# Attention heads: the values products of two key tiles placed together, after the odd tile's second pair of scores

## The chip, the cores and the metric

The kernel runs on one core of a Trainium2 chip. The metric is device time in microseconds of one execution of the whole program; lower is better. The profile is one further execution of the same program, taken with the hardware profiler.

## What is computed

The program is a small network of six blocks over x of shape 2 x 2048 x 256: a mixture of experts, full attention, the mixture of experts again, a gated recurrence, causal attention with relative positions, and the recurrence again. The change touches only the full attention, 16 heads of 16 features in each of 2 batches, so 32 heads in all:

```python
q = x @ Wq.T * (1.0 / jnp.sqrt(jnp.asarray(D, x.dtype)))
k = x @ Wk.T
v = x @ Wv.T
scores = jnp.einsum('bqhd,bkhd->bhqk', q, k)          # S = 2048 queries and keys, Dh = 16
attn = jax.nn.softmax(scores, axis=-1)
out = jnp.einsum('bhqk,bkhd->bqhd', attn, v).reshape(B, S, D)
return out @ Wff.T + bff
```

## The kernel before

`heads_full_stage` (from L1472's loop helper to the end of the stage) goes over the 32 heads. Each head has KT = 16 key tiles of 128 keys and NQ = 4 blocks of 512 queries. Four engines each run a program of their own and meet at semaphores.

**Maxima, two heads ahead.** TensorE multiplies a tile of 128 queries with 1024 keys (`far`, L1646): two matmuls of 48 rows, one on array rows 0 to 47 and one on rows 64 to 111, into two adjacent banks of PSUM. Banks 0 to 3 make two such slots. VectorE takes the maximum of the 128x1024 result (L1742), 32 times a head; a `far` may start when VectorE has emptied the slot of two `far`s before (`m_free`). A small maximum over these (L1748), a 128x16 transpose on TensorE (`row`, L1653) and a copy on ScalarE (L1704) turn them into one row per head. SyncE writes it under the queries as a 49th contraction row.

**Scores and exponentials.** For key tile `kt` and query block `n`, `score` (L1618) multiplies 49x128 keys with 49x512 queries into one of only three banks, 4 to 6 (`bank`, `FULL_BANKS = 3`). The even blocks use array rows from 64 on, the odd ones from 0. ScalarE takes the exponential into `pT` (L1699), which has room for four key tiles. Score unit u = 4 kt + n may start when the exponential of unit u - 3 has ended (`p_ready`).

**Values products.** `weighted` (L1627) multiplies the four 128x512 blocks of exponentials of a key tile with the 128x32 values (16 features, one column of ones for the denominator, padding), each into its own 32 partitions of bank 7, and accumulates over the 16 tiles. In fp32 each of the four is two matmuls in the profile, so eight per key tile. It waits for the tile's fourth exponential. Its end raises `pv_done`, which lets ScalarE overwrite the slot in `pT` four tiles later, GpSimd copy the values of a later head (L1600), SyncE load queries and keys, and, once per head, ScalarE copy bank 7 out (`out`, L1709).

**The order on TensorE** is written out by hand in `body`, per key tile:

```python
score(i, q, kt, 3)
score(*after, 0)
far; far                      # the next two of ring
score(*after, 1)
score(*after, 2)
weighted(i, q, kt)
if left and kt == ROW_KT: row(...)      # ROW_KT = 11
```

where `after` is the next key tile (or tile 0 of the next head). So the first three scores of a tile are made during the tile before it. ScalarE's and VectorE's programs follow the order of the scores and of the `far`s. The outer loop runs over groups of four heads, the last group is written out, and the last head has no `far`s left; head 30 has only 22.

Of the kernel before, what the change touches and what calls it, by code (L numbers as in the profile page):

```python
# [1478 lines left out]
def heads_full_stage(k, ctx, V):  # L1479
# [3 lines left out]
    with ExitStack() as local:  # L1483
# [46 lines left out]
        def segment(q, left):  # L1530

            out = [(1, (q + 1) % 4, p) for p in range(AHEAD, SEG)] if left else []
            if left > 1:
                out += [(2, (q + 2) % 4, p) for p in range(AHEAD) if p != ROW_AT]
            return out
# [3 lines left out]
        with nc.Block() as block:  # L1539
# [65 lines left out]
            def _(pe):  # L1605
                def score(i, q, kt, n):
                    u = kt * NQ + n
                    b = bank(q, u)
                    if u >= FULL_BANKS:
                        pe.wait_ge(p_ready, PC + i * NS + u + 1 - FULL_BANKS)  # L1610
                    else:
                        former = max(v for v in range(NS) if bank((q + 3) % 4, v) == b)
                        pe.wait_ge(p_ready, PC - NS + i * NS + former + 1)
                    if u == 0:
                        pe.wait_ge(row_loaded[q], 32 * (i // 4 + 1 + q // 3))
                    base = TILE_ROWS * ((n + 1) % 2)
                    at = slice(base, base + PARTS_ROWS + 1)
                    nc.tensor.matmul(k.psum[:, b, :], k_sb[at, q, kt * P:(kt + 1) * P],  # L1618
                                     q_sb[at, q, n * BLK:(n + 1) * BLK], start=True, stop=True).then_inc(s_ready, 1)

                def weighted(i, q, kt):
                    pe.wait_ge(p_ready, PC + i * NS + (kt + 1) * NQ)
                    if kt == 0:
                        pe.wait_ge(vh_ready, i + 1)
                        pe.wait_ge(o_free, i + 1)
                    for j in range(NQ):
                        last = nc.tensor.matmul(k.psum[32 * j:32 * j + VP, 7, :], vh[:, q % 2, kt, :],  # L1627
                                                pT[:, kt % 4, j * BLK:(j + 1) * BLK],
                                                start=(kt == 0), stop=(kt == KT - 1), skip_group_check=True)
                    last.then_inc(pv_done, 1)  # L1630

                def far(i, q, p):
                    u = far_of(p)
                    if u == 0:
                        pe.wait_ge(qk_loaded[q], 16 * LOADS * (i // 4 + 1))
                    if p - 2 == ROW_AT:
                        pe.wait_ge(row_done, i + 1)
                    elif p >= 2:
                        pe.wait_ge(m_free, 2 + i * NF + far_of(p - 2) + 1)
                    else:  # L1640
                        pe.wait_ge(m_free, 2 + (i - 1) * NF + far_of(SEG + p - 2) + 1)
                    t, b = u // 2, slot(q, p)
                    for c in range(2):
                        at = slice(TILE_ROWS * c, TILE_ROWS * c + PARTS_ROWS)
                        lo = (u % 2) * WIDE + c * BLK
                        last = nc.tensor.matmul(k.psum[:, b + c, :], q_sb[at, q, t * P:(t + 1) * P],  # L1646
                                                k_sb[at, q, lo:lo + BLK], start=True, stop=True)
                    last.then_inc(m_ready, 1)

                def row(i, q):  # L1650
                    pe.wait_ge(mm_ready, i + 1)
                    pe.wait_ge(m_free, 2 + i * NF + NF)
                    nc.tensor.matmul(k.psum[0:KT, slot((q + 1) % 4, ROW_AT), 0:P], mm[:, q % 2, :], negI[:, :],  # L1653
                                     start=True, stop=True).then_inc(row_ready, 1)
# [13 lines left out]
                def body(i, q, left):  # L1668
                    ring = segment(q, left)
                    for kt in range(KT):  # L1670
                        score(i, q, kt, 3)
                        after = (i, q, kt + 1) if kt + 1 < KT else (i + 1, (q + 1) % 4, 0)
                        more = kt + 1 < KT or left
                        if more:
                            score(*after, 0)
                        for ahead, h, p in ring[2 * kt:2 * kt + 2]:
                            far(i + ahead, h, p)
                        if more:
                            score(*after, 1)
                            score(*after, 2)  # L1680
                        weighted(i, q, kt)
                        if left and kt == ROW_KT:
                            row(i + 1, (q + 1) % 4)

                full_heads_loop(pe, body)

            @block.scalar
# [614 lines left out]
```

## Time and profile before

| | |
|---|---|
| three runs | median 5137.71 us, 5130.94 to 5146.51 |
| profiled execution | 5147.41 us, span 5145.7 us |
| TensorE busy | 4600.3 us (89%) |
| VectorE busy | 3222.8 us (63%) |
| ScalarE busy | 2505.1 us (49%) |
| GpSimd busy | 549.0 us (11%) |
| full attention's heads | 723 to 2172 us of the span |

In the profile PE is TensorE's matmuls, PEld its weight loads, DVE VectorE, ACT ScalarE, POOL GpSimd, SP SyncE; L1627 is line 1627 of the kernel. A busy PE isn't PE at its peak, since matmuls are pipelined and their ends modelled. PEclk is the clock granted to TensorE as a share of full speed (1.00 is 2.4 GHz, 0.50 is 1.2 GHz). In a row of the timeline "x4" merges four instructions that follow each other, and the bracket at the end is idle time of the engine ahead of the row, with what ended it.

### The profile page before, as it was taken

How to read it: one execution, taken by the hardware profiler on the slowest of the kernel's cores; microseconds unless marked ns; L12 is line 12 of the kernel's file. 1: busy time of each engine (PE TensorE's matmuls, PEld its weight loads, DVE VectorE, ACT ScalarE, POOL GpSimd, SP SyncE). 2: the span in 40 equal slices, each digit the busy share in tenths (PEclk: the TensorE clock that was granted, in tenths of full speed). 3: DMA queues.
4: the chain of work that ended last, by engine and by line, in shares of the span. 5: the costliest groups of instructions: out<-in, count | busy, mean ns of one | idle time of the engine just before them, and what ended most of it. 6: DMA issues, size and time to landing. Idle time of an engine off the chain costs nothing. (4 is left out here: it accounts for less than half of the span.)

```text
span 5145.7 us, 82390 instructions
## 1 busy us (share of the span) xinstructions
PE 4600.3 (89%) x24752; PEld 2446.0 (48%) x24752; DVE 3222.8 (63%) x5811; ACT 2505.1 (49%) x4917; POOL 549.0 (11%) x536
## 2 busy tenths in 40 slices
PE   7999869999999999889998957699999999997688
PEld 6888723333333333258886534333444344343345
DVE  6655668888888888356664334476666666673132
ACT  3222327777777777613222211166666666664122
POOL 2322100000000000013322012200000000000000
PEclk9999969999999999789999988799999999998789
DMA  2000411111111111020000043443333333322401
GB/s 77 0 0 1 138 49 42 41 40 42 37 37 39 41 42 29 9 80 1 0 0 18 1 94 79 92 119 91 91 90 91 91 91 90 91 72 46 75 22 33
DMA packets 357225, 272.92 MB, mean 53 GB/s; under 512 B 218440, under 2 KB 314200, under 8 KB 350168
## 3 DMA queue, kind: packets, MB, share of 16 engines
q1 hardware_dynamic: 344536, 225.94, 17.5%
q0 software_dynamic: 12288, 41.95, 2.8%
q8 instruction: 213, 3.49, 0.3%
q14 instruction: 188, 1.54, 0.1%
HBM read 173.97 MB, written 106.95 MB: 55 GB/s over the span
## 5 line engine op out<-in xcount | busy, mean ns | idle before, releaser
L1742 DVE TENSOR_REDUCE full_tops<-psum 128x1 f32<-128x1024 f32 x1024 | 1206.7, 1219 | 254.2 <-PE psum L1646 254.0
L1699 ACT ACTIVATE full_probs<-psum 128x512 f32<-128x512 f32 x2048 | 1067.3, 603 | 356.1 <-PE psum L1618 322.1
L1203 ACT ACTIVATE big<-psum 128x512 f32<-128x512 f32 (+3 forms) x1280 | 644.7, 532 | 473.2 <-PE psum L1103 267.7
L1240 DVE TENSOR_REDUCE big<-psum 128x1 f32<-128x512 f32 (+4 forms) x1152 | 650.3, 581 | 211.6 <-PE psum L1132 201.1
L1618 PE MATMUL psum<-full_q,full_k 49*128 49x512 f32 x2048 | 665.1, 486 | 54.2 <-ACT full_probs L1699 38.3
L1618 PEld LDWEIGHTS psum<-full_q,full_k 49*128 49x128 f32 x2048 | 292.2, 191 | 655.0 <-ACT full_probs L1699 589.9
L1627 PE MATMUL psum<-full_probs,full_vh 128*32 128x512 f32 x4096 | 573.2, 633 | 0.7 <-ACT full_probs L1699 0.7
L1114 PE MATMUL psum<-big 128*32 128x512 f32 (+3 forms) x2560 | 493.8, 549 | 0.0
L1095 PE MATMUL psum<-big 97*128 97x512 bf16 (+3 forms) x1280 | 443.3, 359 | 53.9 <-ACT big L1203 39.0
L1646 PE MATMUL psum<-full_k,full_q 48*128 48x512 f32 x2048 | 406.3, 461 | 66.2 <-DMA full_k<-qk_split 39.6
L1132 PE MATMUL psum<-big 96*128 96x512 bf16 (+4 forms) x1152 | 373.9, 353 | 17.1 <-ACT big L1189 13.5
L275 POOL TENSOR_TENSOR moe_h_lo<-moe_h,moe_h_hi 128x512 fp32r<-128x512 f32 x224 | 290.2, 1296 | 664.4 <-ACT moe_h_hi L388 664.4
L312 PE MATMUL psum<-moe_x_hi,moe_w_hi 128*128 128x512 f32 x896 | 353.3, 394 | 3.9 <-DVE moe_h L454 3.8
L312 PE MATMUL psum<-moe_x_lo,moe_w_hi 128*128 128x512 f32 x896 | 351.1, 392 | 0.0
L312 PE MATMUL psum<-moe_x_hi,moe_w_lo 128*128 128x512 f32 x896 | 349.9, 391 | 0.0
L450 DVE TENSOR_TENSOR moe_ts<-psum,moe_sg 128x512 f32<-128x512 f32 x224 | 154.6, 690 | 297.0 <-ACT moe_sg L396 296.7
L388 ACT CAST moe_h_hi<-moe_h 128x512 fp32r<-128x512 f32 x224 | 138.9, 620 | 383.6 <-DVE moe_h L454 383.6
L1646 PEld LDWEIGHTS psum<-full_k,full_q 48*128 48x128 f32 x2048 | 202.9, 195 | 217.1 <-DVE full_tops L1742 149.8
L396 ACT ACTIVATE moe_sg<-psum 128x512 f32<-128x512 f32 x224 | 133.7, 597 | 261.2 <-PE psum L312 259.7
L326 PE MATMUL psum<-moe_w_hi,moe_h_hi 128*128 128x256 f32 x896 | 256.0, 286 | 2.5 <-POOL moe_h_lo L275 2.5
L326 PE MATMUL psum<-moe_w_lo,moe_h_hi 128*128 128x256 f32 x896 | 253.7, 283 | 0.0
L326 PE MATMUL psum<-moe_w_hi,moe_h_lo 128*128 128x256 f32 x896 | 253.6, 283 | 0.0
(171 smaller groups left out, 6043.4 us busy)
## 6 DMA issues: line engine op xcount, KB each, us to landing
arena<-bias_tiles SPq DMA_DIRECT2D x32, 1280.0 KB, 6.6
band_probs<-xn POOLq DMA_DIRECT2D x64, 320.0 KB, 4.8
band_probs<-xT POOLq DMA_DIRECT2D x64, 320.0 KB, 4.4
qk_split<-qkvf_parts SPq DMA_DIRECT2D x32, 512.0 KB, 4.2
full_q<-qk_split SPq DMA_DIRECT2D x64, 256.0 KB
full_k<-qk_split SPq DMA_DIRECT2D x64, 256.0 KB
big<-qk_parts SPq DMA_DIRECT2D x224, 64.0 KB
qk_parts<-big SPq DMA_DIRECT2D x32, 384.0 KB, 2.9
```

The source lines that it names most:

```text
L312: last = nc.tensor.matmul(k.psum[:, 2 * (u % 2) + kind, :], W[wp][:, e, kind, c, m * P:(m + 1) * P], (xhi, xlo)[xp][:, half, c, :], start= ...
L326: last = nc.tensor.matmul(k.psum[:, 4 + pair, t2 * D:(t2 + 1) * D], (h, h_lo)[xp][:, (half + e) % 2, c, t * P:(t + 1) * P], W[wp][:, e, 2, ...
L1095: last = nc.tensor.matmul(k.psum[:, bank, 0:hi - lo], k_sb[0:ROW + 1, q, kt * P:(kt + 1) * P], q_sb[0:ROW + 1, q, lo:hi], start=True, stop ...
L1114: last = nc.tensor.matmul(k.psum[32 * j:32 * j + VP, 7, lo - j * BLK:hi - j * BLK], vh[:, q % 2, kt, :], pT[:, kt % 4, lo:hi], start=(kt = ...
L1132: last = nc.tensor.matmul(k.psum[:, b + (c - lo) // BLK, 0:e - c], q_sb[0:ROW, q, t * P:(t + 1) * P], k_sb[0:ROW, q, c:e], start=True, sto ...
L1203: nc.scalar.activation(pT[:, kt % 4, lo:hi], k.psum[:, 4 + u % SCORE_BANKS, 0:hi - lo], ACT.Exp).then_inc(p_ready, 1)
L1240: nc.vector.reduce_max(mx[:, r, t, slot:slot + 1], src, AX_X).then_inc(m_free, 1)
L1618: nc.tensor.matmul(k.psum[:, b, :], k_sb[at, q, kt * P:(kt + 1) * P], q_sb[at, q, n * BLK:(n + 1) * BLK], start=True, stop=True).then_inc( ...
L1627: last = nc.tensor.matmul(k.psum[32 * j:32 * j + VP, 7, :], vh[:, q % 2, kt, :], pT[:, kt % 4, j * BLK:(j + 1) * BLK], start=(kt == 0), st ...
L1646: last = nc.tensor.matmul(k.psum[:, b + c, :], q_sb[at, q, t * P:(t + 1) * P], k_sb[at, q, lo:lo + BLK], start=True, stop=True)
L1699: nc.scalar.activation(pT[:, kt % 4, n * BLK:(n + 1) * BLK], k.psum[:, bank(q, u), :], ACT.Exp).then_inc(p_ready, 1)
L1742: nc.vector.reduce_max(mx[:, q % 2, u // 2, u % 2:u % 2 + 1], src, AX_X).then_inc(m_free, 1)
```

## The change

On even key tiles no values product is issued. On odd ones, at the place where `weighted(i, q, kt)` stood, those of the even tile before it and of the odd tile follow one another. Nothing else differs: the number of instructions, the buffers and the waits of each instruction are the same.

```diff
                         if more:
                             score(*after, 1)
                             score(*after, 2)
-                        weighted(i, q, kt)
+                        if kt % 2:
+                            weighted(i, q, kt - 1)
+                            weighted(i, q, kt)
                         if left and kt == ROW_KT:
                             row(i + 1, (q + 1) % 4)
```

## Rows read from the trace of the kernel before

**Rows 1.** The page's costliest groups: xcount | busy, mean ns of one | idle before.
```profile
L1742 DVE TENSOR_REDUCE full_tops<-psum 128x1 f32<-128x1024 f32 x1024 | 1206.7, 1219 | 254.2 <-PE psum L1646 254.0
L1699 ACT ACTIVATE full_probs<-psum 128x512 f32<-128x512 f32 x2048 | 1067.3, 603 | 356.1 <-PE psum L1618 322.1
...
L1627 PE MATMUL psum<-full_probs,full_vh 128*32 128x512 f32 x4096 | 573.2, 633 | 0.7 <-ACT full_probs L1699 0.7
```

**Rows 2.** Timeline of PE, one ordinary key tile, and the two passes of its values product.
```profile
1408.52 0.50 PE L1618 MATMUL psum<-full_q,full_k 49*128 49x512 f32 x2
1408.86 0.75 PE L1646 MATMUL psum<-full_k,full_q 48*128 48x512 f32 x4
1409.44 0.76 PE L1618 MATMUL psum<-full_q,full_k 49*128 49x512 f32 x2
1410.13 1.07 PE L1627 MATMUL psum<-full_probs,full_vh 128*32 128x512 f32 x8
...
1410.58 0.61 PE L1627 MATMUL psum<-full_probs,full_vh 128*32 128x512 f32 x4
...
1411.12 0.50 PE L1618 MATMUL psum<-full_q,full_k 49*128 49x512 f32 x2
```

**Rows 3.** Timeline of PEld (TensorE's weight loads), the same key tile.
```profile
1408.63 0.19 PEld L1646 LDWEIGHTS psum<-full_k,full_q 48*128 48x128 f32 x2
1409.10 0.19 PEld L1646 LDWEIGHTS psum<-full_k,full_q 48*128 48x128 f32 x2 [0.28 <-DVE full_tops L1742]
1409.21 0.19 PEld L1618 LDWEIGHTS psum<-full_q,full_k 49*128 49x128 f32 x1
1409.70 0.18 PEld L1618 LDWEIGHTS psum<-full_q,full_k 49*128 49x128 f32 x1 [0.30 <-ACT full_probs L1699]
1410.13 0.16 PEld L1627 LDWEIGHTS psum<-full_probs,full_vh 128*32 128x32 f32 x8 [0.24 <-ACT full_probs L1699]
```

**Rows 4.** Timeline of ACT, the same key tile.
```profile
1409.05 0.60 ACT L1699 ACTIVATE full_probs<-psum 128x512 f32<-128x512 f32 x1 [0.54 <-PE psum L1618]
...
1409.05 2.06 ACT L1699 ACTIVATE full_probs<-psum 128x512 f32<-128x512 f32 x4 [0.54 <-PE psum L1618]
1411.66 0.60 ACT L1699 ACTIVATE full_probs<-psum 128x512 f32<-128x512 f32 x1 [0.54 <-PE psum L1618]
```

**Rows 5.** Timeline of DVE around the same key tile.
```profile
1406.69 2.35 DVE L1742 TENSOR_REDUCE full_tops<-psum 128x1 f32<-128x1024 f32 x2 [0.47 <-PE psum L1646]
1409.30 2.35 DVE L1742 TENSOR_REDUCE full_tops<-psum 128x1 f32<-128x1024 f32 x2 [0.25 <-PE psum L1646]
```

**Rows 6.** Timeline of PE: one head, first values products of it and of the next.
```profile
1362.39 1.06 PE L1627 MATMUL psum<-full_probs,full_vh 128*32 128x512 f32 x8
...
1404.92 1.07 PE L1627 MATMUL psum<-full_probs,full_vh 128*32 128x512 f32 x8
```

**Rows 7.** Timeline: tile 11 of that head and the next tile, PE and ACT.
```profile
1391.07 1.06 PE L1627 MATMUL psum<-full_probs,full_vh 128*32 128x512 f32 x8
...
1393.58 0.50 PE L1646 MATMUL psum<-full_k,full_q 48*128 48x512 f32 x2 [0.35 <-ACT full_rows L1704]
...
1394.25 1.07 PE L1627 MATMUL psum<-full_probs,full_vh 128*32 128x512 f32 x8
...
1393.29 0.24 ACT L1704 CAST full_rows<-psum 16x128 fp32r<-16x128 f32 x1
```

**Rows 8.** Timeline of ACT and PE where the loop over four heads ends.
```profile
1444.94 0.49 PE L1618 MATMUL psum<-full_q,full_k 49*128 49x512 f32 x2
1445.36 1.07 PE L1627 MATMUL psum<-full_probs,full_vh 128*32 128x512 f32 x8
...
1456.45 1.08 ACT L1699 ACTIVATE full_probs<-psum 128x512 f32<-128x512 f32 x2 [5.37 <-issue]
```

**Rows 9.** Busy time by stretch: us; PE, PEld, DVE, ACT, POOL; PEclk, DMA share, GB/s.
```profile
1362.39:1404.92 42.53, 42.07 (x260) 15.23 (x259) 37.77 (x34) 33.78 (x68) 0.40 (x1) 1.00 0.14 42
2104.00:2127.00 23.00, 18.83 (x109) 5.61 (x101) 0.00 (x0) 18.46 (x38) 0.00 (x0) 1.00 0.03 7
2127.30:2171.00 43.70, 40.95 (x130) 10.34 (x129) 0.00 (x0) 22.00 (x44) 0.00 (x0) 0.50 0.00 1
```

**Rows 10.** Timeline of PE in the last head, which has no maxima work.
```profile
2122.23 1.06 PE L1627 MATMUL psum<-full_probs,full_vh 128*32 128x512 f32 x8
2124.83 1.06 PE L1627 MATMUL psum<-full_probs,full_vh 128*32 128x512 f32 x8
...
2127.53 1.94 PE L1627 MATMUL psum<-full_probs,full_vh 128*32 128x512 f32 x8
2129.39 1.22 PE L1618 MATMUL psum<-full_q,full_k 49*128 49x512 f32 x3
...
2131.59 1.94 PE L1627 MATMUL psum<-full_probs,full_vh 128*32 128x512 f32 x8
```

## The prediction, made before any run of the change

> **What bounds the kernel now.** I began with the page's costliest groups. In the heads VectorE's maxima are busy 1207 us, ScalarE's exponentials 1067 us, the values products 573 us [rows 1]; VectorE and ScalarE both have idle time in front of them that ends with a TensorE score or maximum product. So neither streams freely. The timeline of one key tile tells why. Tiles follow each other every 2.60 us (1408.52 to 1411.12 [rows 2]), though four exponentials need only 2.06 us from first start to last end, or four steps of 0.49 = 1.95 us ((2.06 - 0.60)/3 = 0.49 [rows 4]), and two maxima 2.35 us [rows 5].
>
> The reader should see a ring. The exponential of (kt,3) starts at 1409.05 and ends at 1409.65 [rows 4]. The third score of the next tile, which needs its bank, loads at 1409.70 [rows 3] (+0.05), the values product loads at 1410.13 [rows 3] (+0.43), the next score stands at 1411.12 [rows 2] (+0.99) and its exponential at 1411.66 [rows 4] (+0.54). With 0.60 for the exponential that is 0.05 + 0.43 + 0.99 + 0.54 + 0.60 = 2.61 us, the spacing measured. The last head shows the same spacing with no maxima work at all (2122.23 to 2124.83 [rows 10]), so this ring, not TensorE's work and not VectorE, sets the pace. ScalarE has three exponentials in hand when the values product is coming: they last 3 x 0.49 = 1.46 us after 1409.65, and the product ends at 1411.12, 1.47 us after it. The cover is used up to the last 0.01 us, and the 0.54 that follows is ScalarE's idle time.
>
> VectorE has its own limit nearby: two slots. It idles 0.25 us a tile [rows 5], and the second maximum product of a tile already waits for it (end 1406.69 + 2.35 = 1409.04, load 1409.10 [rows 5, 3]).
>
> **What the change does, step by step.** No instruction is added or removed; eight matmuls move behind six score and maxima instructions of a later tile.
>
> 1. *The double block.* One product occupies TensorE 0.99 us up to the next load; its second pass starts 0.45 after the first (1410.13, 1410.58) and the next load comes 0.54 after that [rows 2]. If the second product follows like another pass, the block takes 0.99 + 2 x 0.44 = 1.87 us; at worst 2 x 0.99 = 1.98. I take 1.87, since the weights of all eight matmuls are loaded within 0.16 us [rows 3], ahead of the second pass.
>
> 2. *ScalarE's ring over two tiles.* In the odd tile: 0.05 + 0.43 + 1.87 + 0.54 + 0.60 = 3.49 us from one fourth exponential to the next, for the cover is still three banks, 1.46 us, against 1.87. In the even tile no product stands in the way and ScalarE runs at its own pace, 4 x 0.49 = 1.96. Sum 5.45, against 5.21 before. What is gained in the even tile (0.65) is less than what is lost in the odd (0.88).
>
> 3. *VectorE's ring, which is longer still.* Count from the load of the even tile's first maximum product, x. Its reduction starts at x + 0.67 (1408.63 to 1409.30 [rows 3, 5]); the two reductions end at x + 3.02. Only then is the slot free for the odd tile's second maximum product: load at x + 3.08 (0.06 as above). TensorE is in order, so the odd tile's scores 1 and 2 and the double block stand behind it. Scores: + 0.34 (1409.10 to 1409.44 [rows 3, 2]); double block: + 0.32 to 0.42 after the first of two scores that stand together (1444.94 to 1445.36, 0.42; from the second of them, some 0.1 later, 0.32 [rows 8]). Here both have array rows of their own and start together, so I take 0.33. Then 1.87, and 0.11 from the score's load to the next maximum product's (1408.52 to 1408.63 [rows 2, 3]). Sum 3.08 + 0.34 + 0.33 + 1.87 + 0.11 = 5.73 us for two tiles, 0.52 over 5.21. The fourth exponential of the odd tile is ready by about x + 2.97 (score wait and steps of 0.49 laid out from x + 0.43), so it isn't late. Bounds: 5.45, if VectorE's ring doesn't bite, and 5.73 + 0.09 + 0.11 = 5.93.
>
> 4. *Count.* Heads 0 to 30 have 31 x 8 = 248 pairs. Around each of seven loop ends TensorE is stalled by ScalarE (5.37 us of issue [rows 8]) and then slow, about two pairs each, where I count 0.3 instead of 0.52: 234 x 0.52 + 14 x 0.3 = 126 us.
>
> 5. *Head ends and the row.* A head takes 42.53 us [rows 6], of which 16 x 2.605 = 41.68 are tiles; tile 11 takes 3.18 (1391.07 to 1394.25), 0.57 over, for the row copy on ScalarE at 1393.29 [rows 7], and the remaining 0.28 is ScalarE's copy of bank 7 at the head's end. With ScalarE's ring 0.28 shorter than VectorE's, the copy is hidden: about -0.22 x 24 = -5 us. The row copy now delays a far product that has slack; between nothing and 0.35 a head, I take -0.15 x 31 = -5. The load queue on SyncE, GpSimd's copy of the values and the storing wait for a head's last `pv_done`, which stands where it was. The even product's slot in `pT` comes free a tile later, but the exponentials that need it are the third tile on: hidden.
>
> 6. *Last head.* Before it runs mostly at half clock (4.06 us a tile, 2127.53 to 2131.59 [rows 10]). A double block in place of two takes away one drain; between -5 and +5, I take 0.
>
> 7. *The clock.* In ordinary heads TensorE is busy 42.07 of 42.53 us and the granted clock is 1.00, 2.4 GHz; in the last head it was busy 18.83 of 23.0 us, kept 2.4 GHz that long, then fell to 0.50, 1.2 GHz, and stayed, busy or not (40.95 of 43.70) [rows 9]. The new pair has 1.87 us of dense products and then 5.73 - 1.87 = 3.86 us with four pairs of maxima products and the scores, broken by waits for exponentials and for VectorE: thinner than any stretch of an ordinary head, about as thin as the last head. So I expect some falls. A fall costs (4.06 - 2.60) = 1.46 us a tile at low clock, and two to three tiles pass until recovery, as after a loop end: about 3.5 us. Bounds: none, 0; one in every head and more, 100 us. I take ten, 35 us, the low side, because the dense block comes back every pair.
>
> Sum: 126 - 5 - 5 + 0 + 35 = **+151 us**. Against the profiled execution's 5147.4 us this is 5298; it lies 9.7 us above the median of the three runs, so the median should come to about **5288 us**.
>
> The skill bears on step 1. The Trainium skill, "TensorEngine Tiling (Array Packing)", Tiling Modes, says that changing the tiling mode drains TensorE. The trace agrees in kind: 0.54 against 0.45. By that rule alone the change saves a drain at either end of a block and the result would be that of the first rival below.
>
> **Rivals.**
>
> *Faster: TensorE's own work bounds.* TensorE is 99% busy by its records [rows 9]. Grouping spares a switch into and out of the block, 0.12 us at the exit (0.99 + 0.87 against 1.98) and about 0.1 at the entry. If the banks and slots bridged the double block, 256 x 0.22 = 56 us would go: 5138 - 56 = 5082. It decides once the cover after the third score is at least 1.87 us. Against it: the cover is 1.46 us [rows 4], and the last head with less TensorE work is no faster [rows 10]. Chance 0.06.
>
> *No difference.* The tiles' spacing is elastic in a way that the single tile doesn't show, and loss and gain cancel: 5138. Chance 0.03.
>
> *Milder: only ScalarE's ring counts.* 5.45 a pair: 248 x 0.24 = 60, with the items of step 5: about 5190. Needs the odd tile's second maximum product to find its slot free. Against: it already waits in the trace before. Chance 0.08.
>
> *Worse: the clock keeps falling.* At 1.2 GHz a double block takes 1.87 + 1.70 = 3.57 us (one is 1.86: 2127.53 to 2129.39 [rows 10]; a further one without drain 1.70). VectorE's ring then gives some 8.4 us a pair. If half the pairs ran so, 124 x 2.7 = 335 us more: about 5590. For it: step 7 and the last head, where the clock never came back. Against: ordinary heads recovered within a few tiles. Chance 0.07. The Trainium skill, "TensorE: Matmul & The Clock Gate", A second HAM failure mode: psum-queue depth-cycling, describes a kernel whose waits between groups of matmuls make the clock swing. No ordinary head of this trace shows it, the last one shows the fall.
>
> **How the numbers follow.** The forecast has the remaining 0.76. Its ends: 126 becomes 234 x 0.38 = 89 if the pair is 5.59, and 234 x 0.72 = 168 at 5.93; the clock adds 0 to 100. So +79 to +258: 5217 to 5396. The range also takes in the milder rival: 5185 to 5400, leaving out the faster side and the bad clock. A measurement of this kernel tells about 0.3% (15 us) from no change. Faster 0.06, same 0.03, slower 0.91.
>
> **What would show it.** Right: pairs of blocks of 16 values matmuls some 5.7 us apart, each 1.87 us long; VectorE idle about 1.1 us before the even tile's first maximum; the odd tile's second maximum product waiting for VectorE; ScalarE with four to five exponentials in a row, then a gap of 0.9; head ends with no extra pause; 42.5 us a head becomes about 46. Step 1 is wrong if the two products are 0.99 apart, step 3 if the pair is 5.45 and the load doesn't wait for VectorE, step 7 if the granted clock in ordinary heads stays 1.00 or swings in each of them. The whole is wrong if pairs come at 5.2 us or less.

## The result and the profile after

The changed kernel takes 5501.74 us (median, 5501.49 to 5504.1) against 5142.11 us of the kernel before in the same series: ratio 1.0713, interval 1.069 to 1.0736. The forecast was slower, 5288 us, at most 5400: the direction held, the size didn't. All ratios below are of undisturbed executions; one execution of the warm kernel's second series took 8482.83 us and stands in none.

The page's costliest groups of the changed kernel, as in [rows 1] (its lines have moved by two: L1744 is the reduction, L1701 the exponential):

```profile
L1744 DVE TENSOR_REDUCE full_tops<-psum 128x1 f32<-128x1024 f32 x1024 | 1189.8, 1216 | 633.9 <-PE psum L1646 633.2
L1701 ACT ACTIVATE full_probs<-psum 128x512 f32<-128x512 f32 x2048 | 1061.8, 610 | 683.4 <-PE psum L1618 643.7
L1627 PE MATMUL psum<-full_probs,full_vh 128*32 128x512 f32 x4096 | 733.0, 853 | 0.0
```

VectorE's and ScalarE's work is within 1.4% of what it was, and their idle time in front of it has grown by 380 and 327 us, nearly all of it waiting for TensorE. The third line tells more: a values matmul lasts 853 ns on average in place of 633. The filled kernel below issues its values matmuls in the same order, and there they last 651: order explains little of it, a slower clock the rest.

The heads' stage as one stretch of the busy-time view (us; PE, PEld, DVE, ACT, POOL; PEclk, DMA share, GB/s), first of the kernel before:

```profile
727.00:2172.40 1445.40, 1382.65 (x8157) 498.53 (x8159) 1158.51 (x1013) 1081.29 (x2105) 12.01 (x30) 0.95 0.12 36
```

and of the changed kernel:

```profile
728.60:2534.40 1805.80, 1662.43 (x8149) 600.22 (x8151) 1138.97 (x1011) 1074.05 (x2101) 12.02 (x30) 0.82 0.10 28
```

The stage is 360 us longer, which is the whole difference. The mean granted clock went from 0.95 to 0.82. With two levels, 1.00 and 0.50, the time at 1.2 GHz is 2 x (1 - PEclk) x length: 2 x 0.05 x 1445 = 145 us before, 2 x 0.18 x 1806 = 650 us after. Below this is called low-clock time. PEclk is rounded to two places, so such a time can be off by 14 to 18 us.

Two pairs of tiles that follow each other in the timeline of PE of the changed kernel show both effects at once:

```profile
1317.14 0.50 PE L1646 MATMUL psum<-full_k,full_q 48*128 48x512 f32 x2 [0.29 <-DVE full_tops L1744]
1317.47 0.40 PE L1618 MATMUL psum<-full_q,full_k 49*128 49x512 f32 x2
1317.81 1.92 PE L1627 MATMUL psum<-full_probs,full_vh 128*32 128x512 f32 x16
1319.66 0.50 PE L1618 MATMUL psum<-full_q,full_k 49*128 49x512 f32 x2
1320.00 0.63 PE L1646 MATMUL psum<-full_k,full_q 48*128 48x512 f32 x4
1320.47 1.85 PE L1618 MATMUL psum<-full_q,full_k 49*128 49x512 f32 x4
1321.91 0.65 PE L1646 MATMUL psum<-full_k,full_q 48*128 48x512 f32 x2
1322.85 0.50 PE L1646 MATMUL psum<-full_k,full_q 48*128 48x512 f32 x2 [0.29 <-DVE full_tops L1744]
1323.19 0.42 PE L1618 MATMUL psum<-full_q,full_k 49*128 49x512 f32 x2
1323.54 3.54 PE L1627 MATMUL psum<-full_probs,full_vh 128*32 128x512 f32 x16
1327.01 0.50 PE L1618 MATMUL psum<-full_q,full_k 49*128 49x512 f32 x2
```

The double block of 1317.81 holds TensorE 1.85 us (to the score at 1319.66), and the next starts 1323.54 - 1317.81 = 5.73 us later; that is the ring of the forecast. The second block is the same work at the low clock: 1327.01 - 1323.54 = 3.47 us. The busy-time view gives the clock, first around another slow double block (1303.44, 3.28 us), then for 5.71 us that hold the fast one of 1317.81, at 2.4 GHz all through:

```profile
1303.00:1306.40 3.40, 3.40 (x20) 0.59 (x16) 1.79 (x2) 1.08 (x2) 0.00 (x0) 0.50 0.13 53
1317.14:1322.85 5.71, 5.42 (x32) 2.13 (x33) 4.61 (x5) 4.13 (x9) 0.00 (x0) 1.00 0.04 14
```

Over the second block itself, 1323.54 to 1327.01, PEclk is 0.52. The weight load of the odd tile's second maxima product shows the wait that step 3 of the forecast rests on, 0.73 us (PEld, of which 0.29 are left in PE's row):

```profile
1317.14 0.19 PEld L1646 LDWEIGHTS psum<-full_k,full_q 48*128 48x128 f32 x2 [0.73 <-DVE full_tops L1744]
```

VectorE's timeline shows its side of the ring, to be held against [rows 5]:

```profile
1314.73 4.61 DVE L1744 TENSOR_REDUCE full_tops<-psum 128x1 f32<-128x1024 f32 x4 [2.61 <-PE psum L1646]
1320.44 4.61 DVE L1744 TENSOR_REDUCE full_tops<-psum 128x1 f32<-128x1024 f32 x4 [1.10 <-PE psum L1646]
1327.79 2.36 DVE L1744 TENSOR_REDUCE full_tops<-psum 128x1 f32<-128x1024 f32 x2 [2.74 <-PE psum L1646]
```

Four reductions without a break, then idle for 1.10 us when the double block ran at 2.4 GHz and for 2.74 when it ran at 1.2. Of the 256 blocks of the stage about 50 follow their predecessor after 5.7 us; most others take 6.0 to 8.2. Counted in the timeline, 177 of the 256 double blocks hold TensorE for more than 1.95 us, 3.24 on average, the others 1.84. So about seven pairs of tiles in ten pay.

### The profile page after: what moved, and what is told of

Its sections match the earlier page's. It is cut to its first block and busy times, and to the rows that moved or that the text cites. A ratio compares the mean times of both kernels' runs of the same rounds, so it can differ in the third digit from the quotient of the medians.

```text
span 5502.4 us, 82390 instructions
## 1 busy us (share of the span) xinstructions
PE 4876.2 (89%) x24752; PEld 2544.2 (46%) x24752; DVE 3206.8 (58%) x5811; ACT 2499.4 (45%) x4917; POOL 549.0 (10%) x536
## 3 DMA queue, kind: packets, MB, share of 16 engines
q8 instruction: 212, 3.47, 0.3%
## 5 line engine op out<-in xcount | busy, mean ns | idle before, releaser
L1744 DVE TENSOR_REDUCE full_tops<-psum 128x1 f32<-128x1024 f32 x1024 | 1189.8, 1216 | 633.9 <-PE psum L1646 633.2
L1701 ACT ACTIVATE full_probs<-psum 128x512 f32<-128x512 f32 x2048 | 1061.8, 610 | 683.4 <-PE psum L1618 643.7
L1618 PE MATMUL psum<-full_q,full_k 49*128 49x512 f32 x2048 | 740.0, 494 | 76.8 <-ACT full_probs L1701 66.8
L1627 PE MATMUL psum<-full_probs,full_vh 128*32 128x512 f32 x4096 | 733.0, 853 | 0.0
L1618 PEld LDWEIGHTS psum<-full_q,full_k 49*128 49x128 f32 x2048 | 323.3, 197 | 626.1 <-ACT full_probs L1701 367.5
L1646 PE MATMUL psum<-full_k,full_q 48*128 48x512 f32 x2048 | 486.3, 467 | 125.5 <-DVE full_tops L1744 66.5
L1646 PEld LDWEIGHTS psum<-full_k,full_q 48*128 48x128 f32 x2048 | 215.3, 198 | 258.3 <-DVE full_tops L1744 174.2
L1627 PEld LDWEIGHTS psum<-full_probs,full_vh 128*32 128x32 f32 x4096 | 137.1, 139 | 375.1 <-issue 198.2
```

What stands on the lines that cost most here:

```text
L1701: nc.scalar.activation(pT[:, kt % 4, n * BLK:(n + 1) * BLK], k.psum[:, bank(q, u), :], ACT.Exp).then_inc(p_ready, 1)
L1744: nc.vector.reduce_max(mx[:, q % 2, u // 2, u % 2:u % 2 + 1], src, AX_X).then_inc(m_free, 1)
```

## The experiments

The theory behind them: the double block outlasts ScalarE's three banks and puts VectorE's second slot ahead of it, which makes a pair of tiles 5.73 us (some 130 us in all); the rest, some 230 us, is the clock, which falls because TensorE's work between double blocks is thin. The rivals were the delay itself, the banks alone, VectorE alone, and a clock with no part in it.

### A tile later, but one by one

```diff
-                        if kt % 2:
-                            weighted(i, q, kt - 1)
-                            weighted(i, q, kt)
+                        if kt:
+                            weighted(i, q, kt - 1)
+                        if kt == KT - 1:
+                            weighted(i, q, kt)
```

> Every values product is issued one key tile later than before the change, at the same place in the order, each by itself; only at a head's end do two stand together. Theory (it is the double block, not the delay, that costs: TensorE is away for 1.87 us where ScalarE has 1.46 us in hand, and the clock falls over the thin stretch between blocks): tiles stay 2.60 us apart, one double block a head adds 0.5 to 3 us, so 5155 to 5240 us. Rival (the delay itself costs, by the slots of the exponentials or by pv_done): 5400 or more, with ScalarE waiting for a values product. Rival (nothing but the number of blocks matters): 5142.

Measured: 5192.72 us, ratio to before 1.0099 (1.007 to 1.0127). The tiles stand 2.60 us apart, as in this timeline of PE:

```profile
1401.00 1.07 PE L1627 MATMUL psum<-full_probs,full_vh 128*32 128x512 f32 x8
...
1403.60 1.06 PE L1627 MATMUL psum<-full_probs,full_vh 128*32 128x512 f32 x8
```

So a product issued a tile late doesn't lengthen a tile; neither the slots of the exponentials nor `pv_done` hold one up. The 1% goes with the one double block of each head: PEclk of the stage is 0.91, 268 us of low clock against 145, and 23 of the 24 falls of the clock in this stage begin 4.6 to 7.2 us behind the start of a double block (six of these blocks stand at loop ends, where the clock fell before the change too).

### The same delay, the blocks apart

In odd tiles, with the change's pair taken apart:

```diff
-                        for ahead, h, p in ring[2 * kt:2 * kt + 2]:
+                        for ahead, h, p in ring[2 * kt:2 * kt + 1]:
                             far(i + ahead, h, p)
+                        if kt % 2:
+                            weighted(i, q, kt - 1)
+                        for ahead, h, p in ring[2 * kt + 1:2 * kt + 2]:
+                            far(i + ahead, h, p)
...
                         if kt % 2:
-                            weighted(i, q, kt - 1)
                             weighted(i, q, kt)
```

> The even tile's values product is issued in the odd tile as in the change, but between the odd tile's two maxima products, in TensorE's wait for VectorE, and the odd tile's own product where it was before. The same delay, the same 16 matmuls for two tiles, two blocks of 0.99 us. Theory: two tiles take about 5.4 us at 2.4 GHz, and the work is spread, so the clock falls seldom: 5190 to 5270 us. Rival (the change costs through ScalarE's banks alone, wherever the blocks stand): as the change, 5450 to 5510. Rival (the delay costs): 5450 or more.

Measured: 5221.5 us, ratio 1.0174 (1.0135 to 1.0213). Timeline of PE, one pair:

```profile
1401.86 1.07 PE L1627 MATMUL psum<-full_probs,full_vh 128*32 128x512 f32 x8
...
1405.69 1.06 PE L1627 MATMUL psum<-full_probs,full_vh 128*32 128x512 f32 x8
1406.68 0.50 PE L1646 MATMUL psum<-full_k,full_q 48*128 48x512 f32 x2
...
1407.35 1.06 PE L1627 MATMUL psum<-full_probs,full_vh 128*32 128x512 f32 x8
```

A pair takes 1407.35 - 1401.86 = 5.49 us (5.4 expected), more than two single tiles, yet the kernel is 280 us faster than the changed one: 0.28 us more a pair, 248 times, is 69 of the 77 us over the kernel before, and PEclk is back at 0.95. The same sixteen matmuls, as late, cost about a fifth as much when they are spread.

### More work in the wait

The changed kernel with repeats of one maxima product, which fill TensorE's 0.73 us wait for VectorE in the odd tile. The semaphore is raised by the last copy.

```diff
-                    for c in range(2):
+                    for c in [0, 1] * copies:
...
-                        for ahead, h, p in ring[2 * kt:2 * kt + 2]:
-                            far(i + ahead, h, p)
+                        for at, (ahead, h, p) in enumerate(ring[2 * kt:2 * kt + 2]):
+                            far(i + ahead, h, p, 3 if kt % 2 and at == 0 else 1)
```

> The changed kernel, with the odd tile's first maxima product issued three times into the same banks (two further pairs of matmuls with the same result), in the 0.73 us in which TensorE waits there for VectorE. More work, none of it on VectorE's or ScalarE's ring. Theory (some 230 of the 360 us are the granted clock, which falls because the stretch between two double blocks is thin): pairs of tiles at 2.4 GHz stay 5.7 us, low clock falls from 650 us of the stage to under 300, time 5380 to 5450 us. Rival (the clock has no part, the rings make it all): 5502 or up to 30 us more. Rival (what counts is the double block's own density, not the thin stretch): low clock unchanged, 5500 to 5530.

Measured: 5297.7 us, ratio 1.0308 (1.0278 to 1.0338). Nearly a thousand matmuls more in the stage, and 204 us less than the changed kernel. The timeline of PE:

```profile
1402.59 1.44 PE L1646 MATMUL psum<-full_k,full_q 48*128 48x512 f32 x8
1403.86 0.40 PE L1618 MATMUL psum<-full_q,full_k 49*128 49x512 f32 x2
1404.19 1.92 PE L1627 MATMUL psum<-full_probs,full_vh 128*32 128x512 f32 x16
...
1409.89 1.92 PE L1627 MATMUL psum<-full_probs,full_vh 128*32 128x512 f32 x16
```

The ring is untouched, 1409.89 - 1404.19 = 5.70 us, and the double block stays at full speed. The gain beat the expectation (5380 to 5450). Its page has the values products at 542.1 us, against 733.0 of the changed kernel; the 191 us between are nearly the whole gain:

```profile
L1627 PE MATMUL psum<-full_probs,full_vh 128*32 128x512 f32 x4096 | 542.1, 651 | 0.0
```

The same values products in the same order, only faster: this shows that the clock is the larger part. The stage:

```profile
726.90:2330.10 1603.20, 1516.96 (x9128) 680.06 (x9127) 1156.79 (x1011) 1075.75 (x2101) 12.02 (x30) 0.94 0.11 32
```

Low clock is 2 x 0.06 x 1603 = 192 us against 650, and the stage is 203 us shorter: 0.44 us lost per us at low clock.

Where the clock still falls supports the theory. Of the 41 double blocks that are still over 1.95 us, 7 stand in the last head, which has no copies, 15 around the ends of heads, and 19 directly behind the row of tile 11, where the pair has a further wait, 0.58 us for ScalarE's copy of the row, that nothing fills. Of the 155 double blocks of tiles 3 to 11 in the other heads not one is slow; in the changed kernel 112 are.

### Half the filling

`2` in place of `3` copies.

> The filled kernel with one extra copy in place of two: half of the filling. Theory (low clock follows how full the thin stretch is): between changed and filled, low clock 250 to 500 us, 5310 to 5430 us, pairs at 2.4 GHz 5.7 us. Rival (a threshold that two copies pass and one doesn't): 5490 to 5510.

Measured: 5426.53 us, ratio 1.057 (1.0546 to 1.0594). In the stage:

```profile
728.00:2452.00 1724.00, 1625.47 (x8637) 647.17 (x8639) 1155.59 (x1011) 1075.88 (x2101) 12.02 (x30) 0.86 0.10 30
```

Low clock 2 x 0.14 x 1724 = 483 us. Against the filled kernel that is 291 us more of it and 121 us more time, 0.42 per us; against the changed kernel 167 us less of it and 82 us less time, 0.49. The price stays between 0.42 and 0.49. One copy gives 75 us, the second 129.

### The same work in the dense place

`3 if kt % 2 == 0 and at == 0 else 1`: the copies stand behind the double block.

> The changed kernel with the same extra work as the filled one (one maxima product of each pair of tiles issued three times), but that of the even tile, which stands right behind the double block where TensorE is dense already, and not in the wait for VectorE. Theory (the clock falls for the thin stretch between the blocks, and the wait in it is what filling cures): the copies add up to 2 x 0.24 us a pair of tiles to the ring and leave the waits where they are, so low clock stays over 450 us of the stage and the time is 5480 to 5620 us. Rival (more work anywhere keeps the clock up): low clock about 200 us as in the filled kernel, 5290 to 5420 us.

Measured: 5506.22 us, ratio 1.0722 (1.0699 to 1.0745), the same as the changed kernel's. The stage:

```profile
729.00:2538.20 1809.20, 1588.04 (x9131) 675.32 (x9131) 1134.19 (x1011) 1095.82 (x2101) 12.01 (x30) 0.88 0.10 28
```

Low clock is 2 x 0.12 x 1809 = 434 us, which the rounding of PEclk doesn't tell from the 450 expected, and far over the 192 of the filled kernel, with the same number of matmuls. So the place of the work matters more than its amount. The amount counts too: it took a third off the low-clock time. It gave nothing back in us: these copies stand on the ring, and pairs at 2.4 GHz take 6.17 us in place of 5.71, some 110 us in 248 pairs, against 216 x 0.44 = 95 us from the clock.

### VectorE with half its work, before and after

In either kernel the maximum goes over the first 512 of each 1024 keys; the other half is left out.

```diff
-                    src = k.psum[:, b:b + 2, :].rearrange("p b n -> p (b n)")
+                    src = k.psum[:, b, :]
```

> The changed kernel with the maximum taken over only the first 512 of each 1024 keys, which leaves out half of VectorE's work (about 0.6 us a reduction instead of 1.22). Theory (VectorE's two slots make two tiles 5.7 us; without that ScalarE's ring of 5.45 is left): pairs at 2.4 GHz 5.4 to 5.5 us, and the thin stretch has no wait for VectorE; 5340 to 5440 us in all. Rival (ScalarE's banks alone set the 5.7): pairs stay 5.7, time 5500. Rival (VectorE is the whole of the loss): pairs 5.2, time 5150 to 5200.

> The kernel before, with the maximum taken over only the first 512 of each 1024 keys, which leaves out half of VectorE's work. Theory (before the change ScalarE's three banks alone set the 2.60 us of a tile, VectorE's slots don't): tiles stay at 2.60 us and the time within 15 us of the kernel before, 5127 to 5150 us. Rival (VectorE bounds the tile): tiles of 2.4 us or less, 5040 to 5090 us.

The changed kernel takes 5307.86 us so (ratio 1.0332, 1.0304 to 1.036), the one before 5139.85 us (1.0012, 0.9998 to 1.0026). Timeline of PE, changed kernel with half the maxima:

```profile
1401.78 1.92 PE L1627 MATMUL psum<-full_probs,full_vh 128*32 128x512 f32 x16
...
1407.21 1.92 PE L1627 MATMUL psum<-full_probs,full_vh 128*32 128x512 f32 x16
```

and the kernel before with half of them:

```profile
1402.29 1.07 PE L1627 MATMUL psum<-full_probs,full_vh 128*32 128x512 f32 x8
...
1404.90 1.07 PE L1627 MATMUL psum<-full_probs,full_vh 128*32 128x512 f32 x8
```

Before the change VectorE sets nothing: 2.61 us a tile with half its load. After it a pair goes from 5.73 to 5.43 us; ScalarE's ring, put at 5.45, is what is left. The time fell further than the 5340 to 5440 expected, since low clock is down to 2 x 0.11 x 1604 = 353 us. The stage is 202 us shorter, of which the ring gives 0.30 x 248 = 74 and the clock, at the price above, 297 x 0.44 = 131. That the clock holds better because the wait for VectorE is gone fits the theory, but here the pair is shorter as well, and this run can't part the two.

```profile
727.40:2331.30 1603.90, 1516.15 (x8148) 614.50 (x8151) 636.62 (x1010) 1052.66 (x2101) 12.01 (x30) 0.89 0.11 32
```

### Keeping the kernel before warm

If work in a wait is free and holds the clock, the kernel before has two places for it: behind each end of the loop over four heads, where ScalarE stands still 5.37 us [rows 8], and the last head [rows 9, 10]. The warm kernel issues one maxima product 18 times in the first and one idle pair of matmuls a tile in the second:

```diff
-                            far(i + ahead, h, p)
+                            far(i + ahead, h, p, 18 if q == 0 and kt == 1 and at == 1 else 1)
...
                             score(*after, 1)
+                            if not left:
+                                idle(q)
                             score(*after, 2)
```

> The kernel before, with TensorE kept busy in its two idle places: the second maxima product of key tile 1 of every first head of four is issued 18 times (in the 4.5 us in which ScalarE stands still at the loop's end), and each tile of the last head has one idle pair of maxima matmuls into banks that nobody reads, in its wait for a bank. Theory (what the clock costs is the thin stretches, and work in a wait is free): no low clock after loop ends, 3 to 5 us less at each of 7, and tiles of the last head 2.6 in place of 4.06 us, 15 us less: 5090 to 5120 us. Rival (the clock doesn't follow such filling, or the copies delay VectorE): 5142 to 5170 us.

Measured: 5115.57 us, ratio 0.9966 (0.9953 to 0.9979). The expectation of no low clock did not hold: the profiled execution (5136.98 us, no better than the kernel before) fell behind some loop ends and ran the last head at 0.50 to its end, though TensorE was now busy 99% of it by its records:

```profile
2102.80:2168.00 65.20, 64.51 (x224) 20.36 (x227) 0.00 (x0) 33.40 (x65) 0.00 (x0) 0.50 0.01 3
```

So its successor has two idle pairs a tile where the real ones had stood, from head 30's tile 12 on:

```diff
+                        if not ring[2 * kt:] and (left == 0 or kt > ROW_KT):
+                            idle(q)
+                            idle(q)
```

> As the warm kernel, but where no maxima products are left (head 30 from tile 12 on and head 31) two idle pairs of maxima matmuls stand in each tile, where the real ones stood, so that TensorE's order is that of an ordinary tile. Theory (the last head falls to half clock because it is thinner than an ordinary tile): the last head's tiles stay 2.6 us apart in every execution, and all 12 to 14 tiles that ran at 4.06 us win 1.4: 5095 to 5115 us, and below the warm kernel. Rival (the clock falls for another reason at the end of the stage): as the warm kernel, 5110 to 5125 us.

> The warm kernel once more beside its successor: its first profiled execution still fell to half clock in the last head and after three of the loop ends. Theory: one idle pair in the last head's tiles isn't enough in every execution, so its times spread more than those of the kernel with two; median 5105 to 5125 us.

Measured: 5114.21 us, ratio 0.9959 (0.9942 to 0.9975), and for the warm kernel again 0.9967 (0.9951 to 0.9982). The two can't be told apart by their intervals, so the expectation that the successor is the faster one is not shown, and its median lies in the rival's range as well as in the theory's. The last 58 us of the stage, kernel before:

```profile
2114.00:2172.00 58.00, 52.35 (x194) 13.79 (x198) 0.00 (x0) 33.49 (x65) 0.00 (x0) 0.61 0.01 3
```

and with the two idle pairs:

```profile
2086.00:2144.00 58.00, 57.26 (x355) 21.96 (x357) 4.83 (x5) 46.34 (x91) 0.00 (x0) 1.00 0.02 4
```

Nearly twice the matmuls, and the last head at 2.4 GHz throughout in this execution. At the loop ends the clock still falls but comes back during the copies. In the timeline of PE of the same run PEclk is 0.50 from 1443.85 to 1444.44, 0.91 over the copies to 1449.18, and 1.00 for the next 10 us:

```profile
1443.85 0.79 PE L1618 MATMUL psum<-full_q,full_k 49*128 49x512 f32 x2
1444.44 4.93 PE L1646 MATMUL psum<-full_k,full_q 48*128 48x512 f32 x38
1449.18 0.54 PE L1618 MATMUL psum<-full_q,full_k 49*128 49x512 f32 x2
```

Both versions are 20 to 23 us (0.3 to 0.4%) below the kernel before.

## Why the prediction was wrong, step by step

**Step 1, the double block:** right. 1.85 us (1.87 taken), so a drain is saved, 0.13 of 1.98. It was never worth anything, because TensorE's work isn't the bound.

**Step 2, ScalarE's ring:** right. 5.43 with VectorE's load halved, 5.45 forecast. The kernel before with the same halving shows that VectorE had no part in the 2.60 us of a tile.

**Step 3, VectorE's ring:** right to the hundredth, 5.73 us, with VectorE idle for 1.10 us and the odd tile's second maxima product waiting for it 0.73 us.

**Steps 4 to 6:** near in sum, but step 5 gained almost nothing. The filled kernel has the change's ring and nearly the clock of the kernel before. Its stage is 1603.2 - 1445.4 = 158 us longer, of which (192 - 145) x 0.44 = 21 are clock: 137 us, where 116 were forecast. One of its heads ran at 2.4 GHz from end to end (timeline of PE: its first double block, those on either side of the row and a wait between them, the first of the next head):

```profile
979.98 1.92 PE L1627 MATMUL psum<-full_probs,full_vh 128*32 128x512 f32 x16
...
1008.54 1.92 PE L1627 MATMUL psum<-full_probs,full_vh 128*32 128x512 f32 x16
1010.28 0.38 PE L1653 MATMUL psum<-full_negident,full_top 128*16 128x128 f32 x2
...
1011.92 0.50 PE L1646 MATMUL psum<-full_k,full_q 48*128 48x512 f32 x2 [0.58 <-ACT full_rows L1706]
...
1014.91 1.92 PE L1627 MATMUL psum<-full_probs,full_vh 128*32 128x512 f32 x16
...
1026.45 1.92 PE L1627 MATMUL psum<-full_probs,full_vh 128*32 128x512 f32 x16
```

A head takes 46.47 us against 42.53, 3.94 more, where 3.79 were forecast (8 x 0.52 less 0.22 and 0.15). The row's pair takes 6.37, which is 0.66 over an ordinary one, while the row cost 0.57 before. Step 5 took 0.15 off for slack in the maxima product that ScalarE's copy of the row holds up; it waits 0.58 us, and the row is no cheaper than it was. At each of the six loop ends where ScalarE stands still (the forecast counted seven) two pairs cost 1.7 us and not 0.6, and the last head is 4 us shorter, inside the bounds of step 6.

**Step 7, the clock:** this term was mis-sized. "I take ten, 35 us, the low side, because the dense block comes back every pair." The term is what is left: 360 - 137 = 223 us. Of these 203 are the measured difference between the changed and the filled kernel, and 21 rest on the price of 0.44. Two numbers in it were wrong in opposite directions. A fall costs about 1.4 us, not 3.5, since it mostly covers one double block (3.24 against 1.84 on average) and is over by the next scores. And falls come in about seven pairs of tiles in ten, not ten times. That the dense block brings the clock back was right and was the wrong comfort: the thin stretch behind it takes the clock away again, and the next dense block then pays. The evidence had been read: the stretch was called as thin as the last head, which had lost its clock. But neither the ten falls nor the upper bound of 100 us had a row behind them.

Of the rivals, "Worse: the clock keeps falling" named what happened and was given 0.07; its 5590 assumed half of the pairs slow all through, 2.7 us each, while in fact about seven in ten are slow in their densest third. That it came within 90 us is partly luck: more pairs, each at half the price. "Milder" and "Faster" are excluded by the pair of 5.73 us.

The Trainium skill, "TensorE: Matmul & The Clock Gate", A second HAM failure mode: psum-queue depth-cycling, says that short idle times between groups of matmuls can make the clock swing and that the throughput lost is in that swing. The trace agrees: no wait of TensorE in an ordinary pair is over 1 us, PEclk of the stage is 0.82, and filling one of these waits brought it to 0.94. Here the loss shows in the matmuls themselves, 853 ns against 651.

What stays open: how much of the low clock after the change depends on the length of a pair of tiles. One and two copies gave 75 and 129 us, which is no straight line; no run varied the length of the pair alone. ScalarE's three banks were not varied in any run; that they set the 2.60 and the 5.43 us rests on the sums and on VectorE's exclusion.

## What to carry to other kernels

Before two pieces of work are put together on an engine that takes its work in order, compare the joined piece with what the engines fed by it have in hand, here 1.85 us against three exponentials of 0.49; a saved drain of 0.13 doesn't weigh against it. Then ask of the rest what is now thin: on TensorE, work moved out of a stretch can cost more through the granted clock than through the waits, here 223 us against 137. The cheap test for it is to repeat harmless matmuls inside a wait; if the kernel gets faster with more work and PEclk rises, the clock is the cause.

## What was not expected of the hardware

- The clock can fall and come back in about seven of ten pairs of tiles for a whole stage, although TensorE is busy 92% of it by its records (1662 of 1806 us). Busy share doesn't show this; PEclk and the mean duration of one matmul (853 against 633 ns) do.
- A low clock is not stable or unstable by itself: in the last head before the change it stayed to the end of the head although TensorE was busy 94% of the time [rows 9], and in the warm kernel although it was busy 99% (64.51 of 65.20 us); after the change it recovered within about one double block.
- About 980 more matmuls in a wait made a kernel 204 us faster (5501.7 to 5297.7); the same number in a dense place left its time as it was (5506.2).
